# A two-layer graph transformer on one core: x loaded through three queues, and weight splitting and edge preparation reordered between VectorE, GpSimd and TensorE

## What is computed

```
xn = layernorm(x)
out = xn @ root + bias                       # and gate, q, k, v: ten groups of 512 columns
for r in range(8):                           # relational convolution
    mask = (edge_type == r)
    sums = segment_sum(xn[src] * mask, dst)
    out += (sums / max(cnt, 1)) @ weight[r]
```

## Time and profile before

| | |
|---|---|
| Median of three runs | 2168.02 us (2167.84 to 2168.52) |
| The profiled execution | 2164.01 us |
| Its span, first to last instruction | 2162.6 us |
| Mean granted TensorE clock | 0.931 |
| TensorE matmul busy | 1891.7 us, 87% of the span |
| VectorE busy | 1138.9 us, 53% |
| GpSimd busy | 785.5 us, 36% |
| ScalarE busy | 438.9 us, 20% |

### The profile page before, as it was taken

The page is one execution under the profiler, slowest core; times in us unless marked ns, Lnnn a source line. Parts: engine busy times, 40 slices in busy tenths (PEclk is TensorE's granted clock), DMA queues, the critical chain, the costliest instruction groups (busy, mean ns, idle before and its releaser), DMA issues.

```text
span 2162.6 us, 30045 instructions
## 1 busy us (share of the span) xinstructions
PE 1891.7 (87%) x10261; PEld 1481.3 (68%) x10261; DVE 1138.9 (53%) x2659; ACT 438.9 (20%) x1004; POOL 785.5 (36%) x619
## 2 busy tenths in 40 slices
PE   4799898997999999999999984533599999979997
PEld 3675566665877877877877763422388888867776
DVE  5867799997354254354443698765631224341121
ACT  3138855551011011011111110010100001110010
POOL 2820000002534643544535683000076553245652
PEclk9899999998999999999999997555699999999999
DMA  3342222223312212222134322000034443012221
GB/s 116 93 139 64 63 68 72 69 68 115 91 39 64 81 50 72 64 62 77 48 126 143 101 59 63 0 1 0 21 113 155 141 131 86 26 54 59 73 64 57
DMA packets 108884, 161.54 MB, mean 75 GB/s; under 512 B 7535, under 2 KB 42285, under 8 KB 108532
## 3 DMA queue, kind: packets, MB, share of 16 engines
q1 hardware_dynamic: 76154, 121.56, 18.8%
q10 hardware_dynamic: 32634, 38.73, 5.4%
HBM read 134.98 MB, written 25.28 MB: 74 GB/s over the span
## 4 chain that ended last, share of the span: by engine, by line
PE 64%; DVE 8%; issue 2%; DVEq 2%; POOL 1%; ACT 1%; ACTq 0%; POOLq 0%
PE ps L402 16%; PE ps L403 16%; PE ps L404 16%; PE ps L1157 8%; PE ps L1526 1%; DVE q_mask L1536 1%; PE ps L1530 1%; PE ps L1839 1%; PE ps L1122 1%; POOL w_hi L245 1%; POOL w_lo L248 1%; PE ps L1068 1%; PE ps L1095 1%; DVE xt_lo L334 1%; DVE stats L306 1%
## 5 line engine op out<-in xcount | busy, mean ns | idle before, releaser
L402 PE MATMUL ps<-w_hi,xt_hi 128*125 128x512 f32 (+1 forms) x1800 | 752.9, 418 | 30.0 <-DVE xt_lo L525 8.4
L245 POOL TENSOR_TENSOR w_hi<-w_stage,zero 128x512 fp32r<-128x512 f32 x288 | 318.0, 1104 | 1251.5 <-PE ps L404 865.5
L403 PE MATMUL ps<-w_lo,xt_hi 128*125 128x512 f32 (+1 forms) x1800 | 711.9, 396 | 0.0
L404 PE MATMUL ps<-w_hi,xt_lo 128*125 128x512 f32 (+1 forms) x1800 | 709.4, 394 | 0.0
L402 PEld LDWEIGHTS ps<-w_hi,xt_hi 128*125 128x125 f32 x1800 | 338.1, 188 | 109.6 <-issue 14.8
L248 POOL TENSOR_TENSOR w_lo<-w_stage,w_hi 128x512 fp32r<-128x512 f32 x288 | 395.5, 1373 | 22.6
L404 PEld LDWEIGHTS ps<-w_hi,xt_lo 128*125 128x125 f32 x1800 | 337.6, 188 | 85.2
L403 PEld LDWEIGHTS ps<-w_lo,xt_hi 128*125 128x125 f32 x1800 | 338.4, 188 | 70.1
L1157 PE MATMUL ps<-a_hi,xn_hi 125*128 125x313 f16 (+1 forms) x640 | 107.4, 299 | 0.0
L1157 PE MATMUL ps<-a_hi,xn_lo 125*128 125x313 f16 (+1 forms) x640 | 107.0, 298 | 0.0
L1526 PE MATMUL ps<-ones_b,q_mask 125*128 125x1 bf16 x800 | 36.1, 168 | 76.4 <-DVE q_mask L1536 73.9
(11 more groups left out here) (353 smaller groups left out, 2255.5 us busy)
## 6 DMA issues: line engine op xcount, KB each, us to landing
w_stage<-in_stream SPq DMA_DIRECT2D x374, 256.0 KB, 2.6
pre<-ring ACTq DMA_DIRECT2D x80, 250.0 KB
a_qk<-pre SPq DMA_DIRECT2D x16, 312.5 KB
a_qkf<-pre ACTq DMA_DIRECT2D x14, 312.5 KB
a_vx<-pre SPq DMA_DIRECT2D x9, 312.5 KB
bias_pre<-in_bias ACTq DMA_DIRECT2D x10, 250.0 KB
nat<-pre SPq DMA_DIRECT2D x2, 1250.0 KB
x<-in_x SPq DMA_DIRECT2D x5, 500.0 KB
```

The lines of the kernel that those rows point to most:

```text
L245: POOL.tensor_tensor(w_hi[:, q, :], w_stage[:, q % NST, :], zero[:].to_broadcast([128, 512]), ALU.add).then_inc(S("hi_done"), 1)
L402: PE.matmul(dst, l_hi, r_hi, start=first, stop=False)
L403: PE.matmul(dst, l_hi, r_lo, start=False, stop=False)
L404: return PE.matmul(dst, l_lo, r_hi, start=False, stop=last)
```

## The change

1. **x**: tile 1 stays on SP's queue, tiles 3 and 4 go to GpSimd's, tiles 0 and 2 stay on ScalarE's.
2. **The head's splits**: ScalarE's splits of chunks 0 to 7 move one m later (two for each m from 2 to 5).
3. **Lower parts**: GpSimd makes `w_lo` for chunks 0 to 7 alone; chunks 8 to 31 go to VectorE, in pieces between the steps of the edge preparation (`split_low_dve`): 8 to 10 between two halves of `key_hot`, 11 to 15 behind `evacuate(0)`, which now stands behind the second half, 16 to 20 behind the totals, 21 to 23 behind `evacuate(1)`, 24 to 31 in `positions`.
4. **f16 copies**: GpSimd subtracts `xn_lo` for each tile behind its last `w_lo`; `natural16` is gone.
5. **Bucket sums**: `key_hot` is made in two halves, and the reduce over 40 buckets in `positions` becomes three additions by halves (40 to 20, 10, 5) and a reduce over 5, with `evacuate(2)` behind the first.
6. **Order**: group 1 stands before `bucket_sums`, group 2 before `pack_buckets`; every `evacuate` is one stage earlier on VectorE, and `evacuate(3)` stands before the memsets and the splits of chunks 32 to 37.

```diff
--- before.py
+++ after.py
@@ -207,8 +207,9 @@
 
     ed_src, ed_dst, ed_typ = (at(n, [P, EC], I32, R_A + 50176 - (i + 1) * 672) for i, n in enumerate(("ed_src", "ed_dst", "ed_typ")))
     bd = at("a0_bd", [128, 128], F32, R_KV + 544)
-    for m in (1, 3):
-        load_x(SP, m)
+    load_x(SP, 1)
+    for m in (3, 4):
+        load_x(POOL, m)
     for c in range(NST):
         load_chunk(c, c)
     for nm, dst in (("src", ed_src), ("dst", ed_dst), ("typ", ed_typ)):
@@ -263,9 +264,13 @@
         POOL.tensor_tensor(w_lo[:, q, :], w_stage[:, q % NST, :], w_hi[:, q, :].bitcast(F32),
                            ALU.subtract).then_inc(S("split_done"), 1)
 
-    with POOL.Fori(0, C_HAND // NSL) as i:
-        for q in range(NSL):
-            split_low(i * NSL + q, q)
+    for c in range(NSL):
+        split_low(c, c)
+
+
+    for m in range(T):
+        POOL.wait_ge(S("xn_hi"), m + 1)
+        POOL.tensor_tensor(xn_lo[:, m, :], nat[:, m, :], xn_hi[:, m, :], ALU.subtract).then_inc(S("xn_lo"), 1)
     POOL.wait_ge(S("split_done"), NST + C_BACK)
     for c in range(C_BACK, C_BACK + (-C_BACK) % NSL):
         split_chunk(c, c % NSL, c // NST + 1)
@@ -479,7 +484,7 @@
         return lambda: stored(groups - 1)
 
     kv = at("a0_kv", [128, 130], F32, R_KV)
-    for m in (0, 2, 4):
+    for m in (0, 2):
         load_x(ALE, m)
     DVE.memset(kv[:], 0.0)
     DVE.memset(bd[:], 0.0)
@@ -557,9 +562,9 @@
         if m >= 2:
             first_high(m - 2)
             first_low(m - 2)
-        if 1 <= m <= 4:
-            split_act(2 * m - 2)
-            split_act(2 * m - 1)
+        if 2 <= m <= 5:
+            split_act(2 * m - 4)
+            split_act(2 * m - 3)
 
     first_turn(0)
     first_turn(1)
@@ -582,15 +587,7 @@
                 first_turn(2 + (k - 2) // 2)
 
     for m in range(T):
-        mk_xn = sig(ALE.activation(xn_hi[:, m, :], nat[:, m, :], ACT.Copy), "act_step")
-
-    def natural16():
-
-        wait(DVE, mk_xn)
-        for m in range(T):
-            DVE.tensor_tensor(xn_lo[:, m, :], nat[:, m, :], xn_hi[:, m, :], ALU.subtract)
-        DVE.drain()
-
+        ALE.activation(xn_hi[:, m, :], nat[:, m, :], ACT.Copy).then_inc(S("xn_hi"), 1)
 
     NB = 626
     adj = at("adj", [P, NBUCKET * NB], I16, R_A)
@@ -640,7 +637,14 @@
     counts = [at(f"counts{i}", [P, NB], I16, R_NAT + i * 1280) for i in range(4)]
     slot_ps = ps[:, 5, 0:2 * NCHUNK]
 
-    def bucket_counts():
+    def split_low_dve(first, last):
+
+        if first == NSL:
+            DVE.wait_ge(S("split_done"), NST + NSL)
+        for c in range(first, last):
+            split_dve(c)
+
+    def bucket_counts(evacuate):
 
         DVE.wait_ge(S("ld_edges"), 48)
 
@@ -664,8 +668,14 @@
         DVE.tensor_tensor(e_key[:], e_key[:], e_tile[:], ALU.add)
         DVE.drain()
 
-        DVE.tensor_tensor(key_hot[:], e_key[:].unsqueeze(1).to_broadcast([P, NBUCKET, EC]),
-                          iota16[0:P, 0:NBUCKET].unsqueeze(2).to_broadcast([P, NBUCKET, EC]), ALU.is_equal)
+        half = NBUCKET // 2
+        for b in (0, half):
+            DVE.tensor_tensor(key_hot[:, b:b + half], e_key[:].unsqueeze(1).to_broadcast([P, half, EC]),
+                              iota16[0:P, b:b + half].unsqueeze(2).to_broadcast([P, half, EC]), ALU.is_equal)
+            if b == 0:
+                split_low_dve(8, 11)
+        evacuate(0)
+        split_low_dve(11, 16)
         DVE.drain()
         kh = key_hot[:].rearrange("p b c -> p (b c)")
         DVE.tensor_tensor_scan(scan[:].rearrange("p b c -> p (b c)"), kh, kh, 0.0, ALU.add, ALU.max)
@@ -716,11 +726,20 @@
     def positions(evacuate):
 
         DVE.tensor_tensor(scan[:], scan[:], b_off[:].unsqueeze(2).to_broadcast([P, NBUCKET, EC]), ALU.add)
+        split_low_dve(24, 27)
         DVE.drain()
         DVE.tensor_tensor(scan[:], scan[:], key_hot[:], ALU.mult)
-        evacuate(1)
-        DVE.drain()
-        DVE.tensor_reduce(e_pos[:], scan[:].rearrange("p b c -> p c b"), AX.X, ALU.add)
+        split_low_dve(27, 31)
+        DVE.drain()
+        n = NBUCKET
+        while n % 2 == 0:
+            n //= 2
+            DVE.tensor_tensor(scan[:, 0:n], scan[:, 0:n], scan[:, n:2 * n], ALU.add)
+            if 2 * n == NBUCKET:
+                evacuate(2)
+                split_low_dve(31, 32)
+            DVE.drain()
+        DVE.tensor_reduce(e_pos[:], scan[:, 0:n].rearrange("p b c -> p c b"), AX.X, ALU.add)
         DVE.drain()
         DVE.tensor_copy(e_posi[:], e_pos[:])
         DVE.drain()
@@ -821,11 +840,14 @@
 
     def beside(dense, evacuate, load_bias, store):
 
-        mk = bucket_counts()
+        mk = bucket_counts(evacuate)
+        split_low_dve(16, 21)
+        dense(1)
         mk = bucket_sums(mk)
-        evacuate(0)
+        evacuate(1)
+        split_low_dve(21, 24)
         mk = group_buckets(mk)
-        dense(1)
+        dense(2)
         mk = pack_buckets(mk)
         positions(evacuate)
         mk = packed_buckets(mk)
@@ -837,10 +859,9 @@
         load_bias(3)
         wait(ALE, mk)
         mk_zero = sig(ALE.activation(adj[:].bitcast(F32), zero[0:P, :].to_broadcast([P, NBUCKET * NB // 2]), ACT.Copy), "act_step")
-        dense(2)
         dense(3)
-        evacuate(2)
-        natural16()
+        evacuate(3)
+        DVE.wait_ge(S("xn_lo"), T)
 
         PE.sem_inc(S("sc_pe"), sc_per)
         zero16 = hot_col[4][0:P, 0:128]
@@ -880,7 +901,6 @@
                     if j == 2:
                         split_act(C_HAND + LEAD + i * KT + k)
             store(i + SC0)
-        evacuate(SC0 - 1)
         for i in range(SC_GROUPS):
             for k in range(KT):
                 for j in range(sc_per):
```

## The result

The changed kernel takes 2178.78 us (median of five, 2174.54 to 2179.52), the kernel before beside it on the same chip 2168.02 (2165.02 to 2170.57). The ratio is 1.0045 with a 95% interval of 1.0031 to 1.0060: slower, by 6.7 to 13 us. The profiled execution took 2174.54 (span 2173.1), 4.2 under its median, as that of before was 4.0 under its own, so the two traces can be set side by side: 10.5 us apart.

What follows compares the result with a forecast made beforehand. TensorE, busy 87% of the span, was taken as the bound, so the scatter phase's start counts. Terms -0.6 + 3.5 - 6.4 + 0.5 + 1.7 + 8.5 = +7.2 on 2168.0 gave 2175.2 us, range 2165 to 2181.

Steps and rivals of the forecast that it cites:

- The forecast case: VectorE's short preparation steps each wait for a GpSimd instruction, and the border opens; 2170 to 2180 us, chance 0.56.
- x: Head: with x on three queues the first dense product comes at 32.3, the middle of 28.3 to 36.1; -0.6 us.
- the full third share: Head: GpSimd's queue takes a third of the five engines; tiles 0 and 1 land at 15.8, tile 2 at 25.6.
- the S of 30.8: Start of the first dense product (S) if GpSimd's copies may use all 16 engines; sum 1.5 us lower.
- The head's splits: Before rows 2 to 4 of group 0 (R): TensorE waits 1.85 for chunk 4 and 1.65 for chunk 6; +3.5 us.
- The hole: TensorE's wait between dense groups 0 and 1 shrinks from 12.2 to 5.8 us, group 1 starting at R+22.7; -6.4 us.
- Rival 1: Edge preparation: GpSimd's xn_lo don't delay VectorE, no hole or slow clock; 2166.8 us, chance 0.20, fast end (2162.8) 0.10.
- The slow clock behind the hole: Group 1: the hole stays over 4 us, so TensorE's half-rate clock still costs its 2.6 us.
- `bucket_sums` and the wait in front of group 3: TensorE: bucket_sums, formerly in the hole, costs +0.5 us behind group 1; VectorE's late evacuate(2) costs +1.7 before group 3.
- The halving wins nothing: VectorE's positions: the shorter reduce gains no time, as VectorE had 8.4 idle us in front of evacuate(2).
- The border: From group 3's end to ScalarE's first scatter step: 12.0 us against 3.5, including 5.3 for store and bias issues; +8.5.
- The sum: All terms together: +7.2 us, giving 2175.2 us in terms of the median.

Runs made afterwards that it cites:

- e2: Changed kernel, with GpSimd's two loads of x issued behind its constants instead of in front; 2177.83 us, ratio 1.0050.
- e1: Changed kernel, with x on two queues (SP and ScalarE) as in the kernel before; 2171.22 us, ratio 1.0025.
- e3: Changed kernel, with GpSimd's five xn_lo held back until VectorE has packed the counts; 2169.50 us, ratio 1.0020.
- e4: Changed kernel, with evacuate(3) moved back behind the memsets and the splits of chunks 32 to 37; 2169.97 us, ratio 1.0016.
- e6: Changed kernel, with evacuate(2) and chunk 31's split in front of the first halving instead of behind it; 2174.58 us, ratio 1.0045.
- e11: Changed kernel, with the old single reduce for the bucket sums, evacuate(2) and chunk 31's split in front of it; 2174.38 us, ratio 1.0045.
- e10: Kernel before, with only the x edit: tiles 3 and 4 from GpSimd, 1 from SP, 0 and 2 from ScalarE; 2167.44 us, ratio 1.0015.
- e5: Changed kernel, with ScalarE's splits of chunks 0 to 7 one m earlier again; 2174.27 us, ratio 1.0039.
- e12: Changed kernel with all repairs, adj zeroed on GpSimd, and chunks 32 to 37 split before VectorE's xn_lo wait and memsets; 2151.58 us, ratio 0.9937.

## Why the prediction came out as it did

The forecast case came about, every term with its sign but one, and the time stayed 3.6 us above the forecast. Point by point, predicted and found:

**x: −0.6, found +1.7.** The step that failed is "I take the middle, 32.3, since the rows speak for neither end". The end of the full third share said tiles 0 and 1 at 15.8 and tile 2 at 25.6; e2, whose constants are early, has tile 0 at 15.91 and tile 2 at 23.34, nearer that end than the middle. And I had counted nothing for what stands behind GpSimd's issue: the drain that waits for its own loads. Both together made 4.5 us against two queues (e1), and the moved splits had won 2.8 of it back (32.91 to 30.07). The Trainium skill (DMA: Bandwidth & Descriptors, on why a DMA increments its semaphore by 16) spreads GpSimd's copy over up to 16 engines. The trace agrees: its queue used 69.8% of all sixteen, where two queues with x use 0.32. But the S of 30.8 that I worked out from it did not come. It left out the late constants, which alone make S 34.6; and its packets were 0.156 us each, while in e2, beside the chunk loads, ScalarE's took 0.22 between 5 and 9 us and 0.29 between 9 and 13, so that tile 2 was read at 23.34 and not at 20.3.

**The head's splits: +3.5, found +5.0.** The two waits were 1.62 and 1.63, as worked out (1.85 and 1.65). The rest is mostly in TensorE's first products: from 34.61 to 40.32 the timeline has 13 of them, 0.44 us each, and 0.23 behind that; before, the slow ones ended at 36, 3.1 behind S. That is 2.6 us more at half rate, 1.3 lost, although the windows there show a granted clock of 1.00. It is in part the luck of this execution: in the six traces with the changed kernel's head (the two of it, e3, e4, e6, e11) the slow stretch lasted from 3.96 to 5.71 us, longest in this one, and S to R was 20.6 to 21.5, that is +4.1 to +5.0. What sets its length, no run tells; in e10, with the old splits, S to R was 16.6, as before.

**The hole: −6.4, found −6.8.** Forecast: `key_hot` 13 behind R and group 1 22.7 behind R; measured 12.8 and 22.45. Two errors cancelled, which is luck: an `xn_lo` takes 2.14 instead of 2.6, and steps with one input gave way as well as `tensor_tensor` steps did, so that the five `xn_lo` were met by the first five steps and the rest of the preparation (66.61 to 68.88) still came behind them. Rival 1 was that the lock would not bite; e3 shows what it would have been worth, 7.6 us at the scatter step. The Trainium skill (SBUF — State Buffer, on the two separate sides) has VectorE and GpSimd share one pair of ports, held for the whole instruction, for VectorE's two-port modes and for steps with two SBUF inputs. The trace agrees on both kinds: `tensor_scalar` with an int32 input, one input only, took 1.82 to 2.19 us here and 0.21 to 0.25 in e3, and that it is quicker there than a `tensor_tensor` of the same size (0.33) fits a two-port mode. I had counted only the second kind.

**The slow clock behind the hole: kept at 2.6, found 1.4 left in this execution, 2.6 to 2.9 in most.** Group 1 took 29.4 us, before 30.5, without a hole 28.0 (e3). In six other traces with the hole of 5.5 us it took 30.5 to 30.9 (the second of the changed kernel, e1, e2, e4, e6, e11), and 29.7 in e5. So the term was right, and the 1.2 that the profiled execution gained here is its own.

**`bucket_sums` and the wait in front of group 3: +0.5 and +1.7, found 2.6 together.** The wait was 2.08. What I had not counted is a slow clock behind it, with which group 3 took 1.7 more. That too is this execution's: in four of the seven traces with this wait group 3 took 28.05 to 28.08. The wait is the change's cost; the 1.7 is not shown to be.

**The halving wins nothing:** right, by e11.

**The border: +8.5, found +9.7.** Chain and order as worked out: e4, which undoes the order alone, brings 7.7 of it back. The term mis-sized is the store and bias issues, 6.9 for 5.3 (5.6 in e4, so their time varies too); the chain in front of them took 6.2 (168.16 to 174.38) for the 6.7 forecast.

**The sum:** +7.2, found +12.7 at the first scatter step and +10.5 at the end. Too low by 2.3 for x, 1.5 for the head, 1.7 for the clock in group 3 and 1.2 for the border, less 1.2 for the clock behind the hole. The second trace of the changed kernel has its first scatter step 11.4 us behind the kernel before's, with 1.6 less for group 3 and 1.3 more for group 1: the two clock terms nearly cancel, and what the forecast had too low in both traces are x, the head and the border.

## What to carry to other kernels

When work is moved to GpSimd to relieve VectorE, ask first which short steps of VectorE run beside it: each may cost a whole instruction of GpSimd's, so a long run of GpSimd work belongs beside VectorE's idle time, not beside its preparation. Work that fills a wait has two sides: it hides itself and it covers what comes next, so before an evacuation is moved forward, look at what must then be done with nothing beside it (here 7.7 us for one line). And a gain in one stage is worth what it is only when nothing in the same edit spends it: what was kept of this change (the head's splits in a new order, lower parts on VectorE, group 1 without a hole) gave 13.6 us once the rest was put right. And before a slow clock is put down to the wait in front of it, a second trace of the same kernel is worth its price: here it showed the same wait without the slow clock.

## What the runs showed of the hardware

- A drain of GpSimd also waits for the DMAs that GpSimd has issued: idle for 12.68 us (12.96 in e10), until its loads of x had landed; with the loads behind it, 0.20 (e2).
- With GpSimd's queue and two others loading rows of 4 KB at once, ScalarE's packets took 0.33 us and GpSimd's 0.28 between 5 and 9 us (ScalarE's 0.22 in the kernel before). Between 9 and 13 us three queues shared what two had had, 31% and 32% of the sixteen engines, and ScalarE's moved 42 packets for 68.
- The lock also takes steps with one input, which I had left out: an int32 `tensor_scalar` 2.0 for 0.25, a normalization of 1024 elements 1.67 for 0.81, and in e12, beside GpSimd's memsets, an f16 `tensor_scalar` 1.50 for 0.28.
- Behind one and the same wait of 2.08 us TensorE's clock fell to 1.2 GHz in three traces (0.50 in 140:142 of the changed kernel's first) and stayed at 2.4 GHz in four (1.00 in the same window of its second).
- TensorE's first products run 0.43 us apart, later ones 0.23, with the granted clock read as 1.00 over both (36:38 of the changed kernel's trace); this lasted from 3.2 to 6.1 us in the fourteen traces.
- GpSimd's memset of 1565 f32 a partition takes 1.35 us (eight in 10.82), not the 2.5 that I had scaled from a small one.
